# A decoder layer with two attentions: probabilities transposed in the array's row halves, scores in quarters, and the second norm's output computed later in the step

## The reference, cut to what matters

```
x = layernorm(x + attn(x))        # 16 heads of 64, softmax over 128 keys
x = layernorm(x + xattn(x, ctx))  # 16 heads of 64, but softmax over the 16 heads of each token
x = layernorm(x + ffn(x))         # rms norm, GELU, light (64) and heavy (512) hidden units
```

## Time and profile before

| | |
|---|---|
| time, median of 3 runs | 426.86 us (426.23 to 427.14) |
| the profiled execution's own time | 427.01 us |
| its span in the trace | 425.1 us |
| mean granted clock of TensorE | 0.993 |
| busy PE / PEld / DVE / ACT / POOL | 399.8 / 347.2 / 288.4 / 239.8 / 146.9 us |

### The profile page before, as it was taken

How to read it: one execution, slowest core, us unless ns; L and a number is a source line. 1 busy time by engine, 2 the same in 40 slices (tenths; PEclk the granted TensorE clock), 3 DMA queues, 4 the chain that set the end, 5 groups by cost and what they waited for, 6 DMA issues and landing times.

```text
span 425.1 us, 14916 instructions
## 1 busy us (share of the span) xinstructions
PE 399.8 (94%) x6068; PEld 347.2 (82%) x6068; DVE 288.4 (68%) x659; ACT 239.8 (56%) x812; POOL 146.9 (35%) x218
## 2 busy tenths in 40 slices
PE   8999899999999999999999999999999998698893
PEld 7797788888998888888988887889888887586772
DVE  4586777775847877668667878658577787437344
ACT  4675575635566565467466747455675565335341
POOL 1542344431414445222424442414234554113022
PEclk9999999999999999999999999999999999999997
DMA  7900113110101112200101022101001101020001
GB/s 276 328 2 8 45 26 90 34 27 8 43 11 30 37 40 70 51 2 17 43 8 46 21 46 76 32 7 36 19 22 39 37 23 47 9 49 25 2 23 53
DMA packets 43594, 19.20 MB, mean 45 GB/s; under 512 B 36544, under 2 KB 40896, under 8 KB 43536
## 3 DMA queue, kind: packets, MB, share of 16 engines
q1 hardware_dynamic: 42688, 16.88, 14.5%
q0 software_dynamic: 560, 1.38, 0.9%
q10 hardware_dynamic: 288, 0.07, 0.1%
HBM read 8.88 MB, written 1.05 MB: 23 GB/s over the span
## 4 chain that ended last, share of the span: by engine, by line
PE 73%; DVE 16%; ACT 4%; issue 4%; POOL 1%; DMA 1%; POOLq 0%; DVEq 0%; SPq 0%; ACTq 0%
PE ps L1133 8%; PE ps L972 7%; PE ps L1062 6%; PE ps L1051 6%; PE ps L944 5%; PE ps L924 5%; PE ps L1043 4%; PE ps L1231 4%; PE ps L926 4%; PE ps L925 4%; PE ps L996 4%; DVE s L844 3%; PE ps L1110 3%; PE ps L963 3%; ACT p L506 2%
## 5 line engine op out<-in xcount | busy, mean ns | idle before, releaser
L506 ACT ACTIVATE p<-ps,neg_max 128x128 f32<-128x128 f32 x256 | 90.0, 382 | 35.9 <-DVE neg_max L720 35.9
L390 POOL TENSOR_TENSOR p<-p,row_inv 128x1024 f32<-128x1024 f32 x32 | 60.7, 1896 | 64.3 <-DVE row_inv L726 64.3
L499 ACT ACTIVATE pt<-ps 128x512 f32<-128x512 f32 x64 | 35.5, 622 | 49.9 <-PE ps L1043 49.9
L506 ACT ACTIVATION_READ_ACCUMULATOR p<-ps,neg_max 128x1 f32 x256 | 57.5, 225 | 0.0
L720 DVE TENSOR_REDUCE neg_max<-ps 128x4 f32<-128x512 f32 x64 | 41.5, 671 | 5.3 <-PE ps L1051 5.3
L1133 PE MATMUL ps<-wo,ot 128*128 128x128 f32 x256 | 32.6, 280 | 6.1 <-DVE ot L765 6.1
L1051 PE MATMUL ps<-kt,qt 64*128 64x128 f32 x512 | 36.9, 284 | 0.0
L1133 PEld LDWEIGHTS ps<-wo,ot 128*128 128x128 f32 x256 | 29.8, 191 | 8.5 <-issue 7.6
L1043 PE MATMUL ps<-ident,p 128*128 128x128 f32 x256 | 35.0, 279 | 1.7 <-POOL p L390 1.3
L765 DVE TENSOR_TENSOR ot<-ps,bv 128x512 f32<-128x512 f32 x32 | 21.5, 673 | 20.8 <-PE ps L1110 19.8
L1062 PE MATMUL ps<-x1t,wq 128*64 128x64 f32 x1024 | 33.8, 224 | 1.9 <-ACT x1t L558 1.1
(11 more groups left out here) (137 smaller groups left out, 846.6 us busy)
## 6 DMA issues: line engine op xcount, KB each, us to landing
v<-v2s SPq DMA_DIRECT2D x256, 32.0 KB
xg<-x_t SPq DMA_DIRECT2D x4, 256.0 KB, 2.7
pt<-w_qk SPq DMA_DIRECT2D x4, 256.0 KB, 4.7
cg<-ctx_t SPq DMA_DIRECT2D x4, 256.0 KB, 2.8
wo<-w_o SPq DMA_DIRECT2D x2, 512.0 KB, 8.8
out<-x2b SPq DMA_DIRECT2D x4, 256.0 KB, 2.2
xres<-x_nat SPq DMA_DIRECT2D x15, 64.0 KB, 1.8
p<-w_v SPq DMA_DIRECT2D x1, 512.0 KB, 6.3
```

What stands on the lines that cost most here:

```text
L390: nc.gpsimd.tensor_tensor(ph, ph, row_inv[:, 8 * half:8 * half + 8].unsqueeze(2).to_broadcast([T, 8, T]), ALU.mult).then_inc(p_ready, 1)
L499: nc.scalar.activation(pt[:, u * BANK:(u + 1) * BANK], bank(T_BANK[u]), ACT.Copy).then_inc(pt_ready, 1)
L506: last = nc.scalar.activation(p[:, hd * T:(hd + 1) * T], bank(S_BANK[q])[:, pos * T:(pos + 1) * T], ACT.Exp, bias=neg_max[:, hd:hd + 1], a ...
```

## The change

Four edits go together. First, each head's transpose becomes two products: the probabilities of queries 0 to 63 pass through the lower 64 rows of the array, those of queries 64 to 127 through the upper 64, each with 64 columns of the identity, and each query half has a bank of its own. ACT's copy puts the 64-element pieces in place. Second, each score product becomes two with 64 columns of weights each, so that the four quarters of the array are in use. Third, x2 of step s is computed in step s+1, behind the first two score maxima; `rms2` on POOL and `normed_x2` on ACT move with it. Fourth, the reciprocal of the second softmax's sum goes behind the second piece of `ot`.

```diff
@@ POOL
+                if s_late(s):
+                    rms2(s - 1)
                 if bc:
                     pool.wait_ge(mv1_ready, s)
...
-                if d:
-                    rms2(s)
@@ ACT
-                    nc.scalar.activation(pt[:, u * BANK:(u + 1) * BANK], bank(T_BANK[u]), ACT.Copy).then_inc(pt_ready, 1)
+                    half, e = u // 2, u % 2
+                    dst = pt[:, half * 8 * T:(half + 1) * 8 * T].rearrange("p (h e q) -> p e h q", h=8, e=2)[:, e]
+                    nc.scalar.activation(dst, bank(T_BANK[u]).rearrange("p (h q) -> p h q", h=8), ACT.Copy).then_inc(pt_ready, 1)
...
-                if not static or s > 2:
-                    normed_x2(s - 1)
                 if a:
                     exponentials(0)
                     exponentials(1)
+                if s_late(s):
+                    normed_x2(s - 1)
@@ DVE
-                        if u == 0 and d and not projecting:
-                            sums2(s)
+                        if d and not projecting:
+                            (sums2, inverse_sums2)[u](s)
                 if a:
                     score_max(0)
                     score_max(1)
+                if not static or s > 2:
+                    x2_out(s - 1)
                 if bc:
                     dve.wait_ge(mm_o, s)
...
-                if d:
-                    x2_out(s)
@@ PE
-                def transpose_p(n, u):
-                    if u % 2 == 0:
-                        pe.wait_ge(p_ready, 2 * n + u // 2 + 1)
-                    for i in range(4):
-                        hd = 4 * u + i
-                        last = nc.tensor.transpose(bank(T_BANK[u])[:, i * T:(i + 1) * T], p[:, hd * T:(hd + 1) * T], ident[:])
-                    last.then_inc(mm_t, 1)
+                def transpose_p(n, half):
+                    pe.wait_ge(p_ready, 2 * n + half + 1)
+                    for i in range(8):
+                        hd = 8 * half + i
+                        for e in range(2):
+                            rows = slice(HALF * e, HALF * e + HALF)
+                            mm = nc.tensor.transpose(bank(T_BANK[2 * half + e])[:, i * HALF:(i + 1) * HALF],
+                                                     p[rows, hd * T:(hd + 1) * T], ident[rows, rows])
+                            if i == 7:
+                                mm.then_inc(mm_t, 1)
...
-                        mm = nc.tensor.matmul(bank(S_BANK[2 * half + i % 2])[:, (i // 2) * T:(i // 2 + 1) * T],
-                                              qt[rows, cols], kt[rows, cols], start=True, stop=True)
+                        for qh in range(2):
+                            first = cols.start + qh * HALF
+                            mm = nc.tensor.matmul(bank(S_BANK[2 * half + i % 2])[qh * HALF:(qh + 1) * HALF, (i // 2) * T:(i // 2 + 1) * T],
+                                                  qt[rows, first:first + HALF], kt[rows, cols], start=True, stop=True)
```

More of the change, by code:

```diff
@@ L267, in run_steps, with s_late @@
                 step(s, s // 2, s // GB, s % GB, s < B, 1 <= s <= B, s >= 2)
+        def s_late(s):
+            return not isinstance(s, int) or s > 2
         def looped(s):
@@ L400, in step @@
                     pool.wait_ge(bd_summed, 1)
-                if d:
-                    rms2(s)
             run_steps(pool, step)
+            rms2(LAST - 1)
             for g in range(B // GB):
@@ L663, in sums2, with inverse_sums2 @@
                 nc.vector.reduce_sum(sum2[:], s2v, AX.X).then_inc(sum2_ready, 1)
+            def inverse_sums2(s):
                 dve.wait_ge(sum2_ready, s - 1)
@@ L755, in step @@
                     sums2(s)
+                    inverse_sums2(s)
                 if phase == 0 and a:
@@ L891, in norm3 @@
                 last.then_inc(out_ready, 1)
+            x2_out(LAST - 1)
             y_out(0)
@@ L897, in _ @@
             sums2(LAST)
+            inverse_sums2(LAST)
             block_diagonal(LAST, 0)
@@ L1074, in step @@
                 if bc:
-                    transpose_p(s - 1, 2)
-                    transpose_p(s - 1, 3)
+                    transpose_p(s - 1, 1)
                 if phase == 0 and a and bc:
@@ L1202, in step @@
                     transpose_p(s, 0)
-                    transpose_p(s, 1)
                 if phase == 3 and not static:
```

## The result

The changed kernel takes 420.27 us (median of 4 runs, 419.54 to 421.26) against 427.00 us of the kernel before on the same chip (4 runs, 426.23 to 427.75): a ratio of 0.984, 95% interval 0.982 to 0.987. That is 6.7 us less, where 8.6 were forecast. The profiled execution took 421.26 us, with a span of 419.4 us. It is the slowest of the four; the spans of the others are 417.7 to 418.5, and why this one is longer is part of what follows.

What follows compares the result with a forecast made beforehand. PE, busy 94%, bounds it, with DVE's nearly equal chain into the first output projection in waiting steps. Second halves 1.5, scores 1.4, waiting steps 5.0, step 16 1.2, less 0.5: 8.6 us, giving 418.3 us; range 414.0 to 422.8.

Steps and rivals of the forecast that it cites:

- What bounds it, and x2 moved: Second scores to first output projection: PE's and DVE's chains nearly equal; moving x2 cuts 6.81 to 6.25 us a step.
- Waiting steps: Steps where the first output projection waits for DVE's `ot`: 5.0 us saved by x2, transposes and scores together.
- Second halves of the transposes: Transposes of heads 8 to 15: 0.63 us each instead of 0.85, or 1.03 between key projections; 1.5 us outside waiting steps.
- First half: Transposes of heads 0 to 7: 1.05 to 0.63 us, but DVE's regrouping copy holds the next projection, so no gain.
- Scores: Score products in quarters: each stretch 1.10 to 1.04 us, 1.4 us saved outside the waiting steps.
- x2's place: x2 between DVE's score maxima and first norm's sum: sum 0.1 to 0.4 us late, 0.5 us lost in all.
- Step 16: x2 and the reciprocal leave DVE's path to `ot` ahead of the longest output projection wait: 1.2 us saved.
- the halves overlap: Rival denied here: transposes' row halves don't overlap or weights set the pace, 1.02 not 0.63 us; 424.2 us, chance 0.10.
- quarters don't run one after the other: Rival denied here: quarters or halves run serially, a score stretch takes 1.86 not 1.04 us; 444 us, chance 0.07.
- x2's place as a wait of 0.3 us in 14 steps: Rival: first norm 0.4 us late, so PE waits 0.3 us for x1; gain 4.6, 422.3 us, chance 0.13.

## Why the prediction was right, and where its sizes were off

The sums below are of the repeated run of the changed kernel, whose time is nearest the median, against the profiled execution of before: distances between the starts of stretches on PE, added over the steps.

- **What bounds it, and x2 moved:** right. Waiting steps 5.0 us forecast; the distance from the second attention's scores to the first output projection fell by 5.0 us in steps 2, 3 and the six that follow with a wait (step 2 gave 0.2 where 0.5 was counted, the other seven 4.8 where 4.5 was). 6.26 us a step in these seven, where 6.25 was forecast. x2 moved alone gave 3.3 of the 5.0 us. The two edits of PE gave the other 1.7 on top of it, and without it 0.0 (halves) and 0.2 us (quarters), as the runs with one alone show.
- **Second halves of the transposes:** 0.63 forecast, 0.64 to 0.65 measured. That this is so close is in part luck: in the trace the starts of successive pairs lie 0.063 us apart, not 0.058, which makes 0.50 for eight, and leaves 0.14 for the change of shape, not 0.17. Where there is no wait, these and the scores of heads 0 to 7 gave 1.6 us, and 0.2 more up to step 1's output projection; 1.9 were forecast.
- **First half:** right that the copy holds L983, and that the halves gain nothing. That they cost something was not seen (below).
- **Scores:** 1.03 for 1.04. For heads 8 to 15, from the first output projection to the transpose of x1, 0.5 us and not 1.0 were left: in waiting steps this distance was 4.76, not 4.80, and went to 4.74 only.
- **x2's place:** the term of 0.5 us was too large. Step 4 loses 0.11 us before the transpose of x1 and 0.05 behind it, as it does with x2 alone moved. Two more steps lose 0.05 each before the second queries, which wasn't followed up. In all others the first norm's sum follows x2 at once and has the time.
- **Step 16:** 1.2 forecast, 0.86 measured. With x2 gone from in front of it, the split came beside POOL's subtraction, and the sum waited 0.36 us for what hangs on that. The step of the prediction that failed is that DVE's chain alone was counted, not the one through POOL and ACT.
- **The term that was missing:** the edits on PE were costed by the time of the products, not by their instructions. From the second queries to the second output projection 1.1 us were lost, in steps 4, 8 and 14. With whole scores this is gone, and the quarters' whole gain with it. But x2 alone moved, with no product more, loses 1.0 us there as well, in steps 13 and 15; so the loss is one of late instructions, and that quarters alone bring it isn't shown.

In all 5.0 + 1.6 + 0.5 + 0.9 - 0.2 - 1.1 = 6.7 us, the 0.2 being what is lost between the transpose of x1 and the second queries; 8.6 were forecast. The stretches left out of this sum cancel: 0.3 us gained up to step 1's second scores, 0.3 lost from the second output projections to the second scores and behind the last of them. No rival came: the halves overlap, x1 is late in step 4 alone, quarters don't run one after the other. One of the rivals' prices was wrong by its own figures, which changes nothing here: x2's place as a wait of 0.3 us in 14 steps takes 4.2 from 9.1 us, a gain of 4.9 and not 4.6.

## What to carry to other kernels

When two chains of nearly equal length meet at an instruction, shortening the one that waits shows up as a longer wait; shortening the other pays until the first takes over (here 3.3 of 5.0 us), and the chain of waits tells which it is. Splitting products to use the array better makes more instructions, which have to be fetched. Where they come late, in a run of small products, a trace shows idle time that no semaphore ended, and the instruction queue's packets beside it. When an operation leaves a place, look at what slides into its time on the engines beside it.

## What was not expected of the hardware

- PE stood idle with no semaphore for 0.1 to 1.0 us at a time, mostly in the middle of runs of 64-column products, and resumed 1.2 to 1.7 us after an instruction packet of 16 KB had landed, in the kernel before too. In the changed kernel the four places lie multiples of 256 instructions of PE apart, to within one.
- TensorE's clock fell to 0.50 after 2.00 us of idle time in three of six profiled executions, and in the kernel before not after 2.9 us.
- POOL's operation on 256 columns took 0.94 to 1.00 us beside a DVE instruction with two inputs in SBUF, and 0.62 beside one with a single one.
- A change of the array's shape cost 0.14 us around transposes: 16 products in 0.64 us, where 8 rounds of 0.063, the distance of their starts, are 0.50. In the kernel before it was 0.20 around the scores of heads 8 to 15 (1.09 us, 8 rounds of 0.112) and 0.16 around the second attention's (1.09 us, 16 rounds of 0.058).
